# Squares of the RMS norm: from GpSimd to VectorE, in the gap behind a tile's first maximum

## The reference, cut to what matters

```python
D_MODEL, N_HEADS, N_KV_HEADS, HEAD_DIM = 512, 16, 4, 32
def rmsnorm(x, w, eps=1e-5):
    inv = jax.lax.rsqrt(jnp.mean(xf * xf, axis=-1, keepdims=True) + eps)
    return (xf * inv).astype(x.dtype) * w
...
xn = rmsnorm(x, norm_w)
q = (xn @ wq).reshape(B, T, N_HEADS, HEAD_DIM)
k = (cond @ wk).reshape(B, S, N_KV_HEADS, HEAD_DIM)
v = (cond @ wv).reshape(B, S, N_KV_HEADS, HEAD_DIM)
scores = jnp.einsum('btgrd,bsgd->bgrts', qg, k) * scale
attn = jax.nn.softmax(scores, axis=-1)
out = jnp.einsum('bgrts,bsgd->btgrd', attn, v)
return residual + out @ wo
```

## Time and profile before

| | |
|---|---|
| median of 3 runs | 4071.2 us (4070.29 to 4072.34) |
| the profiled execution | 4072.93 us, span 4071.2 us, mean granted clock 0.986 |
| busy | PE 3934.5 us, POOL 2366.8, DVE 2326.0, ACT 2022.8 |
| grouped layers | from 2074 us to the end |

### The profile page before, as it was taken

The page is one execution under the profiler, slowest core; times in us unless marked ns, Lnnn a source line. Parts: engine busy times, 40 slices in busy tenths (PEclk is TensorE's granted clock), DMA queues, the critical chain, the costliest instruction groups (busy, mean ns, idle before and its releaser), DMA issues. The chain is left out here.

```text
span 4071.2 us, 51464 instructions
## 1 busy us (share of the span) xinstructions
PE 3934.5 (97%) x18678; PEld 2613.4 (64%) x18678; DVE 2326.0 (57%) x3431; ACT 2022.8 (50%) x2632; POOL 2366.8 (58%) x1193
## 2 busy tenths in 40 slices
PE   9999999998999999999978999999999999999998
PEld 7888888886566656666544555555555555555554
DVE  3221210011755575556637777777777777777775
ACT  3111221121544454444527666666666676666664
POOL 0000000001655565556638998889889889888987
PEclk9999999998999999999979999999999999999999
DMA  5333522233645554555423333333333333333322
GB/s 186 130 134 132 173 97 84 78 116 89 163 125 135 137 139 130 137 133 129 127 70 88 88 88 89 103 98 100 85 103 91 89 101 100 96 90 94 100 78 67
DMA packets 312790, 446.95 MB, mean 110 GB/s; under 512 B 44728, under 2 KB 116408, under 8 KB 312552
## 3 DMA queue, kind: packets, MB, share of 16 engines
q1 hardware_dynamic: 312552, 443.84, 38.7%
HBM read 215.07 MB, written 102.77 MB: 78 GB/s over the span
## 5 line engine op out<-in xcount | busy, mean ns | idle before, releaser
L1968 DVE TENSOR_REDUCE a_max_cols<-a_ps 128x1 f32<-128x512 f32 x1536 | 1036.5, 685 | 265.6 <-PE a_ps L2127 251.4
L1845 ACT ACTIVATE a_probs<-a_ps 128x1024 f32<-128x1024 f32 x768 | 774.2, 1025 | 420.0 <-PE a_ps L2159 415.0
L2127 PE MATMUL a_ps<-a_k_ops,a_q_ops 96*128 96x512 f32 x1536 | 663.7, 434 | 43.0 <-DVE a_max_cols L1968 35.9
L1729 POOL TENSOR_TENSOR a_probs<-a_sums,a_probs 128x1024 f32<-128x1024 f32 x192 | 455.5, 2392 | 208.6 <-DVE x_lo L1978 107.6
L807 POOL MEMSET a_ident<- 128x128 f32 x1 | 0.2, 204 | 975.4 <-issue 975.4
L2127 PEld LDWEIGHTS a_ps<-a_k_ops,a_q_ops 96*128 96x128 f32 x1536 | 292.5, 191 | 366.2 <-DVE a_max_cols L1968 248.1
L2159 PE MATMUL a_ps<-a_q_ops,a_k_ops 128*128 128x512 f32 x1536 | 489.4, 400 | 19.8 <-ACT a_probs L1845 19.7
L1047 DVE TENSOR_REDUCE a_max_cols<-a_ps 128x1 f32<-128x512 f32 x512 | 340.8, 688 | 271.5 <-PE a_ps L1211 271.3
L1731 POOL TENSOR_TENSOR a_sums<-a_probs 128x1024 f32<-128x1024 f32 x192 | 455.7, 2395 | 0.1
L1731 POOL TENSOR_TENSOR a_sums<-a_sums,a_probs 128x1024 f32<-128x1024 f32 x192 | 454.7, 2391 | 0.2
L2175 PE MATMUL a_ps<-a_probs,a_v 128*32 128x512 f32 x3072 | 410.0, 606 | 0.7 <-ACT a_probs L1845 0.6
(11 more groups left out here) (156 smaller groups left out, 7257.0 us busy)
## 6 DMA issues: line engine op xcount, KB each, us to landing
a_k_ops<-k_scratch SPq DMA_DIRECT2D x192, 256.0 KB, 4.4
a_q_ops<-a_qn_hi SPq DMA_DIRECT2D x768, 64.0 KB, 2.0
k_scratch<-cp_out SPq DMA_DIRECT2D x88, 512.0 KB, 2.8
cp_raw<-in_ctx_t SPq DMA_DIRECT2D x64, 512.0 KB, 4.1
a_q_ops<-a_qn_hi SPq DMA_DIRECT2D x256, 128.0 KB, 2.3
x_raw<-out_t SPq DMA_DIRECT2D x25, 1024.0 KB, 7.3
a_q_ops<-a_qn_lo SPq DMA_DIRECT2D x384, 64.0 KB, 2.0
a_x_res<-out_t SPq DMA_DIRECT2D x92, 256.0 KB, 3.1
```

Source lines behind the costliest of these rows:

```text
L1729: pool.tensor_tensor(probs[:, n], sums[:, hp], probs[:, n], ALU.add).then_inc(summed, 1)
L1845: act.activation(probs[:, n], ps[:, 2 * (n % 2):2 * (n % 2) + 2, :], ACT.Exp).then_inc(exped, 1)
L1968: dve.tensor_reduce(max_cols[:, t % 2, col:col + 1], bank(b), AX.X, ALU.max, negate=True)\
L2127: pe.matmul(bank(b), q_ops[0:SHIFT, s, h, q * P:(q + 1) * P], k_ops[0:SHIFT, s, :], start=True, stop=True).then_inc(smax, 1)
```

## The change

In `grouped_layers`, VectorE takes over the three adds and the rest from GpSimd. The adds become two: quarters 0 and 1 get quarters 2 and 3 added in one 128x1024 operation, then quarter 0 gets quarter 1. They stand behind `normalise` in tile 2; the rest stands behind `split_x` in tile 3. `leave_port` now waits for the adds in tile 2 and for the rest in tile 3. In the first tile of batch 0 the adds for batch 1 stand behind maximum 5 and the rest behind maximum 6, and ScalarE rounds behind its fourth exponential instead of behind the third.

```diff
-    SQ = CK + 2
+    SQ = 5
...
-            def sum_squares(n, quarters=range(1, CK)):
-                for k in quarters:
-                    pool.wait_ge(sq_step, n * SQ + k)
-                    pool.tensor_tensor(sq[:, 0, :], sq[:, 0, :], sq[:, k, :], ALU.add).then_inc(sq_step, 1)
-
-            def rest_squares(n):
-                pool.wait_ge(sq_step, (n + 1) * SQ - 1)
-                pool.tensor_tensor(sq_lo[:, :], sq[:, 0, :], as_f32(sq_hi[:, :]), ALU.subtract).then_inc(sq_step, 1)
...
+                if t == 2 and there(it, 2 * T):
+                    pool.wait_ge(sq_step, (it + 2) * SQ + 3)
                 if t == 3 and there(it, 2 * T):
-                    pool.wait_ge(x_split, (it + 2) * CK + 1)
+                    pool.wait_ge(sq_step, (it + 3) * SQ)
...
-                    if isinstance(it, int) and it == 0 and t == 0:
-                        sum_squares(1)
                     sum_probs(it, t, 2)
-                    if isinstance(it, int) and it == 0 and t == 0:
-                        rest_squares(1)
                     sum_probs(it, t, 3)
...
-                    if t == 2 and there(it, 2 * T):
-                        sum_squares(it + 2, range(CK - 1, CK))
                     sum_probs(it, t, 4)
                     sum_probs(it, t, 5)
-                    if t == 1 and there(it, 2 * T):
-                        sum_squares(it + 2, range(1, CK - 1))
-                    if t == 2 and there(it, 2 * T):
-                        rest_squares(it + 2)
...
                     exponential(it, t, 2)
+                    exponential(it, t, 3)
                     if isinstance(it, int) and it == 0 and t == 0:
                         round_squares(1)
-                    exponential(it, t, 3)
...
+            def add_squares(n):
+                dve.wait_ge(sq_step, n * SQ + 1)
+                dve.tensor_tensor(sq[:, 0:2, :], sq[:, 0:2, :], sq[:, 2:4, :], ALU.add).then_inc(sq_step, 1)
+                dve.wait_ge(sq_step, n * SQ + 2)
+                dve.tensor_tensor(sq[:, 0, :], sq[:, 0, :], sq[:, 1, :], ALU.add).then_inc(sq_step, 1)
+
+            def rest_squares(n):
+                dve.wait_ge(sq_step, (n + 1) * SQ - 1)
+                dve.tensor_tensor(sq_lo[:, :], sq[:, 0, :], as_f32(sq_hi[:, :]), ALU.subtract).then_inc(sq_step, 1)
...
+                    if t == 2 and there(it, 2 * T):
+                        add_squares(it + 2)
                     if t == 3 and there(it, 2 * T):
                         split_x(it + 2, 0)
+                        rest_squares(it + 2)
...
                     maximum(it, t, 5)
+                    if t == 0 and first:
+                        add_squares(1)
                     if there(it, t + AHEAD):
                         take_q(*at(it, t + AHEAD))
                     maximum(it, t, 6)
                     if t == 0 and first:
+                        rest_squares(1)
                         turn_squares(1, FB)
```

## The result

| | before | after |
|---|---|---|
| median, both kernels on one chip | 4072.21 us (13 runs) | 4080.56 us (13 runs) |
| ratio | | 1.0020, 95% interval 1.0012 to 1.0028 |
| the profiled execution | 4072.93, span 4071.2 | 4079.68, span 4077.9 |

One of the 13 runs after took 7716.63 us; it is in the median, but not in the ratio, which goes by the undisturbed runs.

A forecast was written before the change was run, and what follows sets the result against it. TensorE, 97% busy, bounds the kernel; other engines cost time only where it waits. Ordinary batches +1.7, batches 10, 12, 14 -0.5, weight-tile batches +6.0 and batch 0 -1.1 sum to +6.1 us: 4077, range 4069 to 4084.

The forecast's parts named there:

- The rule of the gap: Behind `normalise`: each us by which maximum 1 starts later than 1.20 us costs a us of the tile.
- the floor: Length of a tile without any work on the squares, read from batch 22: 19.09 us, used as 19.10.
- Tile 2: Adds in the gap put maximum 1 at 2.48 us, costing 1.28: tile 20.38, 0.2 more than now in ordinary batches.
- Tile 3: `normalise` no longer blocked (-0.64), rest of squares (0.60) takes its place: 0.05 less, tile 20.45.
- Batch 0: First tile +1.75, third tile -2.8, fourth tile 0: together -1.1 us.
- The hold in the first tile: Batch 0: GpSimd's sums hold off VectorE's adds, first add about 2.9 us; TensorE's squares start 1.75 later.
- The fourth tile: Batch 0: GpSimd holds `normalise`, giving back what the clock gives there: 0.
- the third tile: Batch 0: idle 2.91 us and half-rate loss of 1.1 go, 1.28 is added: 21.46 becomes 18.7, -2.8.
- the clock falls: Rival: TensorE's 1.04 us pause in tile 2 lowers the clock, 1.75 us in each of 22, +38: 4115; chance 0.03.
- the border to slower: Whole kernel: above 4079.3 us counts as slower, 8.1 us from no change; slower given 0.33, same 0.58.
- The gap is not free: Denies the first rival: gap free, tile 2 keeps 1.08 in 16 batches, batch 0 another -4: 4050; chance 0.07.
- GpSimd does not end too late: Denies the rival that GpSimd's late end holds `normalise` in tile 3, 0.64 for each of 22, +14: 4091; chance 0.05.

The follow-up runs named there:

- e6: Changed kernel with TensorE adding the squares in four matmuls, no adds or rest on VectorE or GpSimd, low part left out: 4035.92 us, 0.9909.
- e5: Changed kernel without the second of VectorE's two adds, so half of each row's squares is missing; for timing only: 4061.1 us, 0.9974.
- e7: Kernel before (adds on GpSimd), with ScalarE rounding the squares behind exponential 6 of tile 2 and VectorE making the rest in tile 3: 4061.75 us, 0.9974.
- e3: Kernel before, with ScalarE's rounding of the squares in tile 2 moved from behind exponential 4 to behind exponential 6: 4075.86 us, 1.0008.
- e1: Changed kernel with only the adds on VectorE; the rest of the squares back on GpSimd at the end of tile 2: 4070.95 us, 0.9995.
- e8: Changed kernel run and profiled again without an edit: 4081.24 us, 1.0025.
- e4: Changed kernel with GpSimd's sums in batch 0's first tile held back until VectorE's adds and rest are done: 4081.39 us, 1.0019.
- e9: Kernel before the change run and profiled again without an edit: 4072.24 us, 0.9999.
- e10: Adds on VectorE, rest on GpSimd, plus GpSimd held back in batch 0's first tile until adds and rest are done: 4071.28 us, 0.9994.

## Why the prediction was right, and where it was off

**The rule of the gap held.** "Each us by which maximum 1 starts later than 1.20 us behind `normalise` is a us of the tile" was read from one tile without a change in it. The runs put maximum 1 at seven places. The price is the tile without the floor of 19.10, without the 0.23 of each square matmul and, where a_ms_col takes 1.25, without the 0.3 for it (this 0.3 is what tile 3 of the kernel before left over in the prediction; e6, where a_ms_col takes 0.80, needs none):

| tile | maximum 1 behind | less 1.20 | price |
|---|---|---|---|
| e6, tile 2 | 0.81 | none | 0.00 |
| e6, tile 3 | 1.20 | 0.00 | 0.00 |
| e5, tile 2 | 1.73 | 0.53 | 0.55 |
| after, tile 3 | 1.81 | 0.61 | 0.60 |
| e7, tile 3 | 2.33 | 1.13 | 1.08 |
| after, tile 2 | 2.46 | 1.26 | 1.27 |
| e3, tile 3 | 2.92 | 1.72 | 1.72 |

In e1, tile 3 has 1.23 and 0.04. It doesn't matter whether work in the gap or a held `normalise` makes maximum 1 late.

**Tile 2** was forecast at 20.38 in all batches and is 20.35 to 20.39 (20.40 at most in e8), also behind the weight tiles, where nothing was to be gained. The add took 1.22 us, from a row of the same shape with other operands: 1.226.

**Tile 3** was forecast 0.05 shorter, at 20.45. It is 20.47, as before. Maximum 1 did come 0.04 us earlier (1.81 against 1.85), but nothing of it reached the tile, and 21 tiles made 1 us of the forecast's 0.05: too small a difference for the rows that it came from.

**Batch 0.** The hold in the first tile came as told: the first add 2.98 us (forecast "about 2.9"), the tile +1.75. That the tile met its number is in part luck: TensorE's squares start only 1.4 us later against the start of the batch (13.26 against 11.86), where 1.75 was forecast for just this start, and the other 0.35 comes behind it, where TensorE stays longer at the lower clock (the granted clock is 0.50 over the 4 us behind its wait in both profiles after, 0.57 and 0.60 before). On VectorE:

```profile
2127.91 2.98 DVE L1924 TENSOR_TENSOR a_sq<-a_sq 128x1024 f32<-128x1024 f32 x1
2130.93 2.71 DVE L1926 TENSOR_TENSOR a_sq<-a_sq 128x512 f32<-128x512 f32 x1
```

and on GpSimd and TensorE:

```profile
2127.43 5.66 POOL L1722 TENSOR_TENSOR a_sums<-a_probs 128x1024 f32<-128x1024 f32 x2 [12.77 <-ACT a_probs L1828]
```

```profile
2135.59 0.76 PE L2101 MATMUL a_ps<-a_sq_hi,a_ones_r 128*128 128x512 f32 x1 [5.92 <-DVE a_sq_lo L1930]
```

By the Trainium skill (SBUF — State Buffer, "SBUF: two separate sides") the two engines shut each other out for whole instructions, and e4 agrees: with GpSimd held back, the same adds take 1.21 and 0.69. The fourth tile gave 0.4 where the forecast had 0. The prediction took the lower clock behind the 2.91 us of the third tile for 3.5 us long, which is where the window in the earlier trace rows ends; the trace has it at 0.50 until 2191.4, 6.1 us behind the wait. The sum for the third tile does not change by that, as only 2.26 us of it lie in that tile, but the 1.75 us a tile of the rival "the clock falls" come from these 3.5 and are too low.

**What was missing** is 3.0 us in two places that no step of the prediction looked at, as their code doesn't change: the weight tiles (+1.6) and the end (+1.3). Both have a TensorE wait of about 5 us with the lower clock behind it. For the weight tiles that is the whole difference, as e8 and e9 show. At the end it is this wait:

```profile
4056.76 1.94 PE L2191 MATMUL a_ps<-a_probs,a_ones 128*32 128x512 f32 x8 [4.99 <-POOL a_probs L1720]
```

From its end to the end of the kernel are 20.50 and 20.06 us before, 21.14 and 21.07 after, with 4.5 and 3.5 against 5.9 and 5.7 us of the lower clock. The rest of the +1.3 lies ahead of this wait, in tile 3 of batch 23: 16.36 and 17.30 us before, 17.59 twice after, and of these four the first alone has the full clock all through this tile (over 17 us around it the others are granted 0.90). So the two profiles of before agree in the sum, 95.88 and 95.91, by chance, as their parts differ by up to 0.9. Still, the five profiles of kernels with both adds on VectorE (after, e8, e1, e4, e10) have 97.2 to 97.4 for this end and the seven others 95.7 to 96.2. Why is open.

The prediction priced the lost clock only where the change touches a wait (the third tile of batch 0). The step that failed is one it took without saying so, that tiles with unchanged code keep their length: 6.1 and these 3.0 come to 9.1, and the medians lie 8.35 and, in the session of e8, 9.15 apart. The other deviations cancel: +1.0 in tile 3 against -1.0 in tile 2 and batch 0. So the middle of the forecast was 3 us too low, and the outcome came out a little past the border to slower, which had been given 0.33, and not below it, with 0.58.

**The rivals.** The gap is not free (e5, e6). GpSimd does not end too late in the changed kernel: its last sum in tile 2 ends at 3643.75, 1.08 us ahead of `normalise`, against 0.9 forecast; e3 shows what it costs when it does. The clock does not fall behind an idle 1.02: the granted clock is 1.00 from 3626 to 3640 us. In the first rival, "5.1 of POOL's" work should be 5.27 by its own two rows; nothing else rests on it.

**What the prediction didn't see.** It added up the parts and never asked for the parts alone. Its own rows held the answer: GpSimd's rest held `normalise` by 0.64 because GpSimd was late, and the adds made it early.

## What to carry to other kernels

Where one engine reduces what another one produces in two banks, find how far the first reduction may lag before the producer waits; up to there a step in the gap is free, behind it each us is paid in full, whichever engine is idle on average. When a change moves several steps, work out each alone: here the first cured what the second was to cure, and the second only paid. Two extra matmuls on the busiest engine (0.47 us a batch) were cheaper than 1.9 us on a half-idle engine at a place where the busy one waits, if the low part of the sum may go (e6). With the whole sum, the best here was to leave the adds on GpSimd and to round later (e7, 4061.75).

## What the runs showed of the hardware

- TensorE's granted clock fell to the 1.2 GHz level 1.9 to 5.2 us into waits of 5.1 to 5.6 us, and what of it was left behind the wait (3.0 to 6.3 us) cost 0.44 to 0.46 us for each us in the weight tiles. The same kernel repeats this within 0.4 us, and other kernels differ, though the code there is the same: batch 1's tile took 26.22 us with 3.0 left (e6) and 27.72 with 6.3 (e4). What decides where in the wait the clock falls stays open.
- A 16-element tensor_scalar on VectorE (a_ms_col) took 0.17 us with GpSimd idle (batch 0), 1.25 beside GpSimd's sums (in batch 18 it ends at 3651.64, the sums at 3651.60), and 0.80 in e6, where it starts later against them. At 0.80 tile 3 lost nothing, at 1.25 it lost 0.3, and in batch 6 of the changed kernel, where it took 1.53, the tile was 20.75: 0.28 more on both. A small instruction can be a long one, and its price also starts at a threshold.
